# Sorting token choices with one-hot products, and blocks gathered by index, in a six-stage layer stack on one core

## The reference

```python
def _L1_ffn_ref(hidden_states, gate_W, w1_e, w3_e, w2_e, w1_s, w3_s, w2_s):
    flat = hidden_states.reshape(-1, d)
    logits = (flat @ gate_W.T).astype(jnp.float32)
    probs = jax.nn.softmax(logits, axis=-1)
    top_v, top_i = jax.lax.top_k(probs, K)                      # K = 2 of 8
    gates = zeros.at[arange(T)[:, None], top_i].set(top_v)
    g = silu(einsum('td,edf->etf', flat, w1_e))                 # f = 512
    u = einsum('td,edf->etf', flat, w3_e)
    routed = einsum('te,etd->td', gates, einsum('etf,efd->etd', g * u, w2_e))
    gs = silu(einsum('bsd,ndf->nbsf', hidden_states, w1_s))     # 8 shared, f = 64 each
    us = einsum('bsd,ndf->nbsf', hidden_states, w3_s)
    shared = einsum('nbsf,nfd->bsd', gs * us, w2_s) / 8
    return 0.5 * shared + 0.5 * routed
...
x = x + 0.5 * _L1_ffn_ref(_layernorm(x), ...)                   # stages 3 and 5
```

## Time and profile before

| | us |
|---|---|
| median of 3 runs | 1137.5 (1134.17 to 1139.94) |
| the profiled execution | 1141.16 |
| its span (the trace) | 1139.3 |
| mean granted TensorE clock | 0.878 |
| busy in the span: PE / DVE / ACT / POOL | 876.8 / 703.5 / 454.2 / 213.0 |

### The profile page before, as it was taken

The page is one execution under the profiler, slowest core; times in us unless marked ns, Lnnn a source line. Parts: engine busy times, 40 slices in busy tenths (PEclk is TensorE's granted clock), DMA queues, the critical chain, the costliest instruction groups (busy, mean ns, idle before and its releaser), DMA issues.

```text
span 1139.3 us, 21561 instructions
## 1 busy us (share of the span) xinstructions
PE 876.8 (77%) x7803; PEld 684.1 (60%) x7803; DVE 703.5 (62%) x2219; ACT 454.2 (40%) x800; POOL 213.0 (19%) x248
## 2 busy tenths in 40 slices
PE   3599946777665999459899944678888867999992
PEld 3388823444443888349788832344444446888881
DVE  6677666887646776873344436788888555334442
ACT  1133313766621333424355511354555532444550
POOL 7200011000010000347233321000000023613331
PEclk9999965999965999659899976799999866999996
DMA  8970000000000000001300020000000000130003
GB/s 232 298 118 1 2 0 1 2 2 1 2 1 1 1 2 1 1 15 52 106 21 23 22 83 0 1 1 2 1 2 1 2 1 27 51 102 21 24 22 112
DMA packets 43430, 38.69 MB, mean 34 GB/s; under 512 B 6047, under 2 KB 36134, under 8 KB 43328
## 3 DMA queue, kind: packets, MB, share of 16 engines
q1 hardware_dynamic: 38784, 28.84, 9.9%
q0 software_dynamic: 4544, 8.47, 2.3%
HBM read 22.59 MB, written 15.61 MB: 34 GB/s over the span
## 4 chain that ended last, share of the span: by engine, by line
PE 51%; DVE 27%; ACT 8%; POOL 6%; issue 5%; DMA 3%; SPq 0%; DVEq 0%; POOLq 0%
PE bank L1038 7%; PE banks0to L533 6%; POOL l_ffn_sorted L902 5%; PE banks0to L541 4%; DVE score_max L1236 4%; PE bank L552 4%; PE banks0to L1001 4%; PE banks0to L1002 3%; PE bank L1024 3%; PE banks0to L1003 3%; PE bank L1479 2%; ACT stacks_and_choice L1395 2%; PE banks0to L1459 2%; PE banks0to L1464 2%; ACT hidden L1390 2%
## 5 line engine op out<-in xcount | busy, mean ns | idle before, releaser
L775 DVE TENSOR_TENSOR hidden<-silu_gate,banks0to 128x512 f32<-128x512 f32 x110 | 75.5, 688 | 174.7 <-PE banks0to L1003 174.7
L1408 ACT ACTIVATE normed_T<-banks0to 128x1024 f32<-128x1024 f32 x80 | 82.4, 1030 | 105.1 <-PE banks0to L1464 104.9
L939 ACT COPY hidden<-bank 128x512 f32<-128x512 f32 x110 | 64.7, 588 | 144.1 <-PE bank L1024 144.1
L1038 PE MATMUL bank<-l_w,hidden 128*128 (+1 forms) x880 | 119.6, 280 | 3.0 <-ACT hidden L939 3.0
L1038 PEld LDWEIGHTS bank<-l_w,hidden 128*128 128x128 f32 x880 | 112.4, 197 | 13.4 <-issue 4.0
L1236 DVE TENSOR_REDUCE score_max<-banks0to 128x8 f32<-128x1024 f32 x80 | 97.8, 1222 | 20.7 <-PE banks0to L1464 18.6
L908 POOL DMA_INDIRECT l_ffn_results<-normed_T,stacks_and_choice x78 | 76.6, 982 | 176.5 <-DVE normed_T L797 170.5
L189 POOL TENSOR_TENSOR ln_rstd<-ln_var_eps,minus_half 128x4 f32<-128x4 f32 x24 | 24.6, 1026 | 434.6 <-DVE ln_var_eps L182 434.6
L420 DVE SCALAR_TENSOR_TENSOR expert_sum<-bank,gate,expert_sum 128x128 f32<-128x128 f32 x224 | 62.9, 344 | 35.5 <-PE bank L552 35.5
L533 PE MATMUL banks0to<-stacks_and_choice,l_w 128*128 128x128 f32 x512 | 77.8, 297 | 0.0
L933 ACT ACTIVATE silu_gate<-banks0to 128x512 f32<-128x512 f32 x110 | 65.8, 598 | 27.7 <-PE banks0to L1003 24.5
(11 more groups left out here) (240 smaller groups left out, 1790.0 us busy)
## 6 DMA issues: line engine op xcount, KB each, us to landing
l_ffn_sorted<-empty_row SPq DMA_DIRECT2D x2, 2535.0 KB, 23.5
stacks_and_choice<-l_ffn_sorted SPq DMA_DIRECT2D x26, 195.0 KB, 4.6
l_w<-in_L_ffn_w_e SPq DMA_DIRECT2D x2, 2048.0 KB, 13.5
stacks_and_choice<-l_ffn_results SPq DMA_DIRECT2D x8, 512.0 KB, 5.5
l_w<-in_L_ffn_w SPq DMA_DIRECT2D x1, 2048.0 KB, 10.6
l_ffn_results<-normed_T,stacks_and_choice POOLq DMA_INDIRECT x78, 2.3
x_tokens<-in_L_attn_x SPq DMA_DIRECT2D x4, 256.0 KB, 3.8
l_ffn_sorted<-stacks_and_choice,row_places POOLq DMA_INDIRECT x64, 2.3
```

The costliest lines, as they stand in the source:

```text
L775: v.tensor_tensor(net.hidden[:, i % 2, :], net.sil[:, i % 2, :], net.bank[2 + i % 2], ALU.mult).then_inc(self.gated.sem, 1)
L1038: ins = mm(net.bank[5 + i % 2][:, 0:D], net.hiddenT[:, i % 2, f, :], w2, start=(f == 0), stop=(f == FT - 1))
L1408: nc.scalar.activation(net.pT[:, i % 2, :, :], net.scores[:, 1], ACT.Exp).then_inc(self.exps.sem, 1)
```

## The change

It touches stages 2, 3 and 5.

- **Sorting.** The rows are no longer scattered. Instead the list of which choice stands in which sorted row is made as a matrix `sorted`, 128 rows of a block by 39 blocks, twice: choice numbers and gates. A choice with row r of block b contributes a one-hot column for r (`at_row`, DVE L824, 128x128) times a one-hot row for b scaled with the choice's number or its gate (`in_block`, POOL L947, two instructions 128x39 with both factors read from a column). For the choices of 128 tokens that is one product 128x78 (PE L1103); 32 products are summed in one PSUM bank. at_row and in_block have a ring of 8 buffers, which a product makes free. DVE turns the sum into indices (`block_sources`, L927 to L933). SP stores the normalized rows to DRAM in token order (4 DMAs, L756) while the front runs, and POOL gathers one block's 128 rows with one indirect DMA (L957): 12 at once, and then one after each result scatter (L969).
- **Order of the units.** 11 shared units come first (LEAD), then 39 routed ones, then the last 5 shared ones. The sum of each token's two results is added to x after all units.
- **Order of the router.** DVE does gated(0) after L863, gated(1) after L870, and gated(2) and out(0) after L890, between the router's steps. Four small instructions are new (L901 to L904). PE counts after the transposes of unit 0. Then DVE makes 8 at_row after each of units 2 to 5's steps, and PE does 8 products after each of units 3 to 6.
- **PE's wait.** A shared unit's `up` waits for the lower parts of its own group of four tiles, not of all 16.
- **Weights.** 16 of the 18 halves are split in the last pair of stage 2: ACT rounds two halves in each step (L699), DVE subtracts for w1 (L704, 8 times) and POOL for w3 (L704, 8 times). The two shared halves are left to ACT and DVE at the start of stage 3.
- Gone are the filling of the lists at the start, POOL's copies (L893) and the number columns.

DVE in stage 3, from the best two to the first rows of the list. Before, the whole router stands ahead of the first gated product (L775); two places are shown.

The diff, cut to its core:

```diff
-ROW = D + 2
+LEAD = 11
+RING = 8
 BLOCKS = (T * P * TOP + E * (P - 1)) // P
-FETCH = 3
+FETCHED = 12
...
 class ExpertChoice, vector:
+                if self.weights and not more and 1 <= e <= E:
+                    self.weights.make_lower(dve, v, 0, e - 1)
 class ExpertChoice, gpsimd:
+        if self.weights:
+            for e in range(E):
+                self.weights.make_lower(pool, self.net.nc.gpsimd, 1, e)
 class ExpertChoice, scalar:
+                if self.weights and not more:
...
+                    if e < E:
+                        self.weights.round_upper(0, e)
+                    if e >= 1:
+                        self.weights.round_upper(1, e - 1)
...
+class WeightSplit:
...
+    def round_upper(self, w, e):
+
+        self.net.nc.scalar.copy(self.upper(w, e), self.whole[w][:, e, :]).then_inc(self.upper_made[w], 1)
+
+    def make_lower(self, eng, ops, w, e):
+
+        eng.wait_ge(self.upper_made[w], e + 1)
+        ops.tensor_tensor(self.lower_parts[w][:, e, :], self.whole[w][:, e, :], self.upper(w, e),
+                          ALU.subtract).then_inc(self.lower_made, 1)
...
-        self.units = [("shared", t) for t in range(T)] + [("routed", b) for b in range(BLOCKS)]
+        lead = [("shared", t) for t in range(LEAD)]
+        self.units = lead + [("routed", b) for b in range(BLOCKS)] + [("shared", t) for t in range(LEAD, T)]
...
 class TokenChoice, vector:
+        def at_row(c):
+
+            t, k = c // TOP, c % TOP
+            if c >= RING:
+                dve.wait_ge(self.moved.sem, self.moved.at(0, c - RING + 1))
+            v.tensor_scalar(net.at_row[:, c % RING, :], net.row_numbers[:, :], net.choice_row[:, t, k:k + 1], None,
+                            ALU.is_equal).then_inc(self.at_row.sem, 1)
+
+        self.token_choice(dve, chain, lambda: gated(0), lambda: step(0), lambda: step(1))
+        for i in range(2, 6):
+            step(i)
+            for c in range((i - 2) * RING, (i - 1) * RING):
+                at_row(c)
+        self.block_experts(dve, chain)
+        step(6)
+        self.block_sources(dve, chain)
...
 class TokenChoice, gpsimd:
         pool.wait_ge(self.placed.sem, self.placed.at(0, 1))
-        for t in range(T):
-            for k in range(TOP):
-                g.indirect_dma_start(self.sorted_rows, bass.IndirectOffsetOnAxis(ap=net.place[:, t, k:k + 1], axis=0),
-                                     net.rows[:, t, k, :], None).then_inc(self.sent.sem, 16)
+        for c in range(T * TOP):
+            t, k = c // TOP, c % TOP
+            if c >= RING:
+                pool.wait_ge(self.moved.sem, self.moved.at(0, c - RING + 1))
+            for value, dst in ((net.choice_number, net.in_block[:, c % RING, 0, :]),
+                               (net.choice_gate, net.in_block[:, c % RING, 1, :])):
+                ins = g.tensor_scalar(dst, net.block_numbers[:, :], net.choice_block[:, t, k:k + 1],
+                                      value[:, t, k:k + 1], ALU.is_equal, ALU.mult)
+            ins.then_inc(self.in_block.sem, 1)
...
+        for landed in self.stored:
+            pool.wait_ge(landed.sem, landed.at(1))
+        pool.wait_ge(self.indexed.sem, self.indexed.at(0, 1))
+        for b in range(FETCHED):
+            fetch(b)
         for b in range(BLOCKS):
...
+            if b + FETCHED < BLOCKS:
+                fetch(b + FETCHED)
...
 class TokenChoice, tensor:
+        def move(c):
+
+            pe.wait_ge(self.at_row.sem, self.at_row.at(0, c + 1))
+            pe.wait_ge(self.in_block.sem, self.in_block.at(0, c + 1))
+            mm(net.bank[7][:, 3 * P:3 * P + 2 * BLOCKS], net.at_row[:, c % RING, :],
+               net.in_block[:, c % RING, :, :].rearrange("p i b -> p (i b)"), start=(c == 0),
+               stop=(c == T * TOP - 1)).then_inc(self.moved.sem, 1)
...
+            if 3 <= i < 3 + T * TOP // RING:
+                for c in range((i - 3) * RING, (i - 2) * RING):
+                    move(c)
```

More of the change, by code:

```diff
@@ L756, in vector @@
         for t in (self.front.xn, self.front.lower, self.front.logit, self.router_steps, self.selected, self.placed,
-                  self.experts, self.gated, self.out, self.rows_lower, self.added):
+                  self.experts, self.gated, self.out, self.rows_lower, self.at_row, self.indexed, self.added):
             t.prime(dve)
         chain = Chain(dve, self.router_steps.sem, self.router_steps.at(0, 0))
-        def lower_weights(g):
-            if self.splits:
-                for k in self.share("vector", g):
-                    self.lower_weight(dve, net.nc.vector, k)
-        self.front.vector(dve, chain, lower_weights)
-        self.token_choice(dve, chain)
-        assert chain.n == self.router_steps.per, chain.n
+        if self.first:
+            for w in range(2):
+                self.weights.make_lower(dve, v, w, E)
+        self.front.vector(dve, chain)
         def gated(i):
@@ L795, in out, with step @@
                 dve.wait_ge(self.returned[slot].sem, self.returned[slot].at(turn))
-            dve.wait_ge(self.fetched[n // FETCH].sem, self.fetched[n // FETCH].at(1))
-            v.tensor_scalar(net.results[:, slot, :], y, net.block_rows[:, n, D + 1:D + 2], None,
+            v.tensor_scalar(net.results[:, slot, :], y, net.sorted[:, 1, n:n + 1], None,
                             ALU.mult).then_inc(self.out.sem, 1)
-        gated(0)
-        for i in range(len(self.units) + 1):
+        def step(i):
             if i + 1 < len(self.units):
@@ L808, in vector @@
                 out(i - 1)
+        def at_row(c):
[12 more added lines that the diff above has]
+        self.block_sources(dve, chain)
+        assert chain.n == self.router_steps.per, chain.n
+        for i in range(7, len(self.units) + 1):
+            step(i)
         groups = T // GROUP
@@ L915, in scalar @@
             t.prime(act)
-        if self.splits:
-            self.weights_upper.prime(act)
-            act.wait_ge(*self.loaded)
-            act.wait_ge(*(self.before or (net.choice_const, 1)))
-        def upper_weights(g):
-            if self.splits:
-                for k in self.share("scalar", g):
-                    nc.scalar.copy(self.upper(k % 2, k // 2), (self.w1, self.w3)[k % 2][:, k // 2, :]
-                                   ).then_inc(self.weights_upper.sem, 1)
-        self.front.scalar(act, upper_weights)
+        if self.first:
+            act.wait_ge(*self.before)
+            for w in range(2):
+                self.weights.round_upper(w, E)
+        self.front.scalar(act)
         def silu(i):
@@ L962, in tensor @@
             pe.wait_ge(net.const, 4)
-        for t in (self.front.xnT_psum, self.front.logits, self.counted, self.up, self.turned, self.down, self.rowsT):
+        for t in (self.front.xnT_psum, self.front.logits, self.counted, self.up, self.turned, self.down, self.rowsT,
+                  self.moved):
             t.prime(pe)
         self.front.tensor(pe)
-        pe.wait_ge(self.front.lower.sem, self.front.lower.at(0, T // GROUP))
-        pe.wait_ge(*self.loaded)
-        pe.wait_ge(self.weights_split, 2 * NE)
+        pe.wait_ge(*self.weights.loaded)
+        pe.wait_ge(self.weights.lower_made, 2 * NE)
         expert = {}
```

205 lines of the change are left out of this document (108 added, 97 removed).

## The result

| | before | after |
|---|---|---|
| median of 7 runs, us | 1139.94 (1134.17 to 1140.73) | 1130.69 (1128.88 to 1131.97) |
| ratio | | 0.9928 [0.9912, 0.9944] |
| the profiled execution, us | 1141.16 | 1131.04 |
| its span, us | 1139.3 | 1129.3 |

The change makes the kernel faster, by 0.72%, some 8 to 9 us. I had said 1116, from a sum of -23.9. The time lies in the range (1104 to 1146), but the gain is less than half of the forecast.

A forecast was written before the change was run, and what follows sets the result against it. No engine bounds the whole: POOL's scatters set the blocks' start, PE the blocks. Stage 2 +1.0, stage 3 -16.9 and stage 5 -8.0 sum to -23.9: 1117.3 profiled, 1113.6 on the median's scale; said 1116, range 1104 to 1146.

The forecast's parts named there:

- A line through the two rows: Sort: POOL's in_block price, from 0.257 (64x1) and 0.526 (128x128), put at 0.34 us for 39 columns.
- p: Sort: us for one in_block, taken as 0.34; the time is about 1117.3 + 128 x (p - 0.34).
- The first rival: Sort: column operands cost what missing columns save, in_block 0.526, sort 35.9 per stage, 1141.1, no change; chance 0.17.
- POOL passes twice: Sort, second rival: comparing and multiplying are two passes, in_block 0.68, sort 45.8, 1161, slower; chance 0.16.
- The bound: Sort: POOL needs 6.0 us per round of eight choices, PE alone 4.8, so POOL bounds it.
- The front: Stage 3, x to first `up`: comes down from 27.13 towards stage 5's 16.13, -9.9 us, once.
- the 1.1: Stage 3's front: delay added for the two shared halves, DVE's products ending at 466.7 where its norm began at 465.57.
- Stage 2's last pair: Weight splitting there costs +1.0 us, of 0 to 5.0; DVE's product alone fits into its 1.21 idle per step.
- The router: Stage 5: gated products, an out and four small steps put its end +3.6 us later, but nothing waits for it.
- The five units: End of stages 3 and 5: five shared units of 2.72 behind the blocks add 13.6 us to the last out.
- The clock: Sort: PE idles 1.2 of each 6.0; a lower clock could add 14 us per stage, taken at nothing.
- The third rival: Sort: POOL keeps DVE's at_row out until its ring is full, 3.6 us per stage, 1124.5; chance 0.12.

The follow-up runs named there:

- pool_forms: The kernel after with 34 more POOL instructions at its end, DVE idle: in_block's form and its neighbours; 1147.87 us in one run, only durations matter.
- all_dve: The kernel after with all in_block made on DVE, eight choices at a time in three instructions, none on POOL; 1100.55 us, ratio to before 0.9656.
- half_dve: The kernel after with in_block's half for the numbers moved from POOL to DVE, the gates' half left on POOL; 1104.13 us, ratio to before 0.9682.

## Why the prediction was wrong

**The step that failed is "A line through the two rows gives ... 0.34 for 39 columns, which I take".** Its two rows are instructions of one operation with a constant (L605 and L1706 of the kernel before), and for that form the line was even somewhat high: 39 columns take 0.278 from start to start. But in_block has a second operation, 0.057, and reads both factors from columns, 0.077 each: 0.49 in all. The columns' price, 0.155, is what the line missed; it is as large as the whole error in p, since the second operation and what the line was too high by (0.06) cancel. A choice took 33.16 / 32 = 1.04 where I had put 0.75; the 0.07 of it for meeting at_row was about right (1.04 less 0.98). The sort took 33.2 instead of 24.3, in both stages: some 18 us of the 23.9.

The first rival, "POOL pays as much as for 128x128", at a chance of 0.17, had the column operands as its cause and so came nearest; but at 0.526 it put them too high, and its time, 1141.1, lies 10 above the measured one. The second, "POOL passes twice", is out: a second operation costs 0.057, not another pass. The Trainium skill (GPSIMD Engine Reference, Performance pitfalls for Q7 kernels) gives about 102 cycles for a small read command; at the page's 1.2 GHz that is 0.085, an estimate. The page says it of kernels written for that engine, not of column operands; if they are read by such commands, the trace agrees within a tenth, since pool_forms has 0.077 for each. By the page p would have been 0.51, an estimate too.

**The bound was right.** POOL sets the sort and PE comes next: taking half of POOL's work away brought 1104, and all of it 1100.6, with PE's round at 4.5 against my 4.8.

**The front** was -8.8 where I had -9.9: 18.30 instead of 17.2. DVE's two products for the shared halves end at 466.32, 2.37 after x, where I had 2.0; that is 0.35 of the 1.1. The rest is a slip in my sum: I added 1.1 as the delay against stage 3's norm before, which began 0.90 after x, but to stage 5's 16.13, in which the norm begins 0.04 after x. In the kernel after the norm begins 2.29 after x in stage 3 and 0.03 in stage 5, and that is the whole of 18.30 less 16.05. POOL's copies, which I left out, brought nothing: stage 5's front is 16.05 after 16.13.

**Stage 2's last pair** cost 0.4, not 1.0. A step of DVE after, beside the earlier trace rows:

```profile
446.37 1.11 DVE L418 SCALAR_TENSOR_TENSOR expert_sum<-bank,gate,expert_sum 128x128 f32<-128x128 f32 x4
447.41 1.37 DVE L704 TENSOR_TENSOR l_w_float32r<-l_w,l_w_float32r 128x512 fp32r<-128x512 f32 x1
448.70 0.47 DVE L404 TENSOR_SCALAR stacks_and_choice<-bank,numbers_column 128x256 f32<-128x256 f32 x1
449.09 1.11 DVE L418 SCALAR_TENSOR_TENSOR expert_sum<-bank,gate,expert_sum 128x128 f32<-128x128 f32 x4
```

DVE's product does take longer beside POOL's, 1.37 instead of 0.69, in most steps. But 1.11 + 1.37 + 0.47 less overlaps is 2.72, just PE's 2.73: the 1.21 idle was enough cover. The 0.4 comes from two other steps: the first that adds takes 2.86 instead of 2.73, and the last but one, in which DVE had idled only 0.90, takes 2.33 instead of 2.03.

**The router** ended 14.57 after the first `up` (947.24 - 932.67), and 15.5 was forecast; the four new steps take 0.6 together (945.18 to 945.78), not 0.8. **From the last product to `turn_rows`**: 6.7, forecast 6.84. **The blocks**: 119.12, forecast 119.0. **The five units**: 12.6, forecast 13.6, as the last two, without an `up` of the next unit on PE, come 2.27 apart and not 2.72. **The additions**: 4.8, forecast 5.4. In stage 5 these make -2.5, against +8.9 from the sort: 6.4 of its -8.0 are gone.

**The clock** was 0.85 in the sort, so PE did fall back to the lower level in parts of it. I took that at nothing, and in the sort it cost at most 0.6 in stage 5, since POOL, the slower one, stood still for only 33.16 - 32.59.

**The third rival** (DVE kept out) didn't come: at_row's longest took 0.374, and a choice's 1.04 is close to the two in_block's 0.98 alone. If one was held up it was in_block: its longest took 0.844, about one at_row more than its median. The Trainium skill (SBUF — State Buffer, Who interferes with whom) has the rule that the second to issue is blocked until the first finishes. These rows agree with it.

**Where the expected gain went**, then: stage 3's front kept it (the weights' part alone gives 10.4 over the whole kernel). The new order saves a tail of 13.4 to 15.2 and needs the blocks to start earlier by five units; POOL's sort let them start only 2.4 us earlier in stage 5 (54.5 after the first `up` instead of 56.9), and sort and order came out at nothing.

## What to carry to other kernels

Price a small instruction in its own form: operands that are read from memory can cost as much as the elements, and a row with constants doesn't show it. A slow side engine does harm where the main engine's queue holds its consumers in a bunch; spread them among independent work, or move the producer, before counting busy shares. And of a change with several parts, run each alone: here one part gave all, and two others lost 19.1 and 10.0 alone and came out near nothing together.

## What the runs showed of the hardware

- GpSimd, tensor-scalar on 128 partitions, fp32, from start to start (pool_forms): 0.278 us with 39 columns, one operation and a constant; +0.057 for a second operation, +0.077 for each operand read from a column, about 0.003 per further column of data.
- VectorE's compare of 128x312 with two broadcast operands took 0.48 (all_dve), so the in_block of eight choices, a compare and two products, took about 1.3 on VectorE (940.48 to 941.79) against 8.1 on GpSimd (32.59 / 4, the kernel after).
- GpSimd's and VectorE's small tensor-scalars side by side: GpSimd's median went from 0.518 (the kernel after) to 0.617 (half_dve), where VectorE had twice as many.
